# TensorE turns the identity 80 times behind each count of tokens and 16 times at the head of each expert stage, results unread

## What is computed

```python
def _L0_ffn_ref(x, router_w, w1, b1, w2, b2):
    logits = jnp.einsum('td,ed->te', xf, router_w)
    top_vals, top_idx = jax.lax.top_k(logits, K)
    probs = jax.nn.softmax(top_vals, axis=-1)
    for e in range(E):
        w = jnp.sum(jnp.where(top_idx == e, probs, 0.0), axis=-1)
        h = jax.nn.gelu(jnp.einsum('td,fd->tf', xf, w1[e]) + b1[e], approximate=False)
        y = jnp.einsum('tf,df->td', h, w2[e]) + b2[e]
        out = out + w[:, None] * y
...
x = x + 0.5 * _L0_ffn_ref(_layernorm(x, axis=-1), ...)
x = x + _L0_attn_ref(_layernorm(x, axis=-1), ...)
x = x + 0.5 * _L0_ffn_ref(_layernorm(x, axis=-1), ...)
...
```

## Time and profile before

| what | value |
|---|---|
| median of 3 runs | 2718.38 us (2714.81, 2718.38, 2722.18) |
| the profiled execution's own time | 2709.58 us |
| its span, first to last instruction | 2707.7 us |
| mean granted TensorE clock over the span | 0.926 |
| TensorE (PE) busy | 2202.2 us, 81% of the span |
| VectorE (DVE) busy | 1953.2 us, 72% |
| ScalarE (ACT) busy | 1418.8 us, 52% |
| GpSimd (POOL) busy | 941.5 us, 35% |
| instructions | 48032 |

### The profile page before, as it was taken

The page is one execution under the profiler, slowest core; times in us unless marked ns, Lnnn a source line. Parts: engine busy times, 40 slices in busy tenths (PEclk is TensorE's granted clock), DMA queues, the critical chain, the costliest instruction groups (busy, mean ns, idle before and its releaser), DMA issues. The chain is left out here.

```text
span 2707.7 us, 48032 instructions
## 1 busy us (share of the span) xinstructions
PE 2202.2 (81%) x15540; PEld 1400.0 (52%) x15540; DVE 1953.2 (72%) x4474; ACT 1418.8 (52%) x2911; POOL 941.5 (35%) x1180
## 2 busy tenths in 40 slices
PE   3399788866978779999999997859776697698986
PEld 3299576756965312232322324659756696433334
DVE  3466688865655679999999974556587565688893
ACT  2166222214645459989899893236443464533333
POOL 4444345553442421111111102554446444223330
PEclk9999898977989969999999998879987798899998
DMA  5122100001220230000000001112211123100001
GB/s 171 40 60 65 50 23 18 17 24 48 66 83 32 83 113 22 21 22 23 20 23 22 20 2 39 35 49 66 64 58 37 56 65 86 46 0 0 0 1 32
DMA packets 110499, 115.42 MB, mean 43 GB/s; under 512 B 21776, under 2 KB 93552, under 8 KB 109488
## 3 DMA queue, kind: packets, MB, share of 16 engines
q1 hardware_dynamic: 91936, 76.13, 9.7%
q0 software_dynamic: 17280, 35.69, 3.9%
q10 hardware_dynamic: 1040, 0.53, 0.1%
HBM read 67.30 MB, written 44.57 MB: 41 GB/s over the span
## 5 line engine op out<-in xcount | busy, mean ns | idle before, releaser
L2060 DVE TENSOR_REDUCE attn_nm<-bank 128x1 f32<-128x1024 f32 x512 | 592.4, 1217 | 27.2 <-PE bank L1802 24.9
L1924 ACT ACTIVATE attn_pT<-bank 128x512 f32<-128x512 f32 x1024 | 554.3, 597 | 64.6 <-PE bank L1818 57.8
L1802 PE MATMUL bank<-attn_K,attn_Q 48*128 48x512 bf16 x1024 | 317.8, 391 | 23.3 <-PEq L1536 16.6
L1837 PE MATMUL bank<-attn_pT,attn_vb 128*32 128x256 f32 x4096 | 328.2, 391 | 10.4 <-issue 10.4
L1818 PE MATMUL bank<-attn_Q,attn_K 51*128 51x512 bf16 x1024 | 318.8, 384 | 1.5 <-DMA attn_Q<-attn_m_parts 1.4
L2004 POOL CAST attn_m_cols<-attn_nm 128x8 bf16<-128x8 f32 x64 | 12.2, 191 | 482.2 <-DVE attn_nm L2060 454.7
L1802 PEld LDWEIGHTS bank<-attn_K,attn_Q 48*128 48x128 bf16 x1024 | 59.2, 94 | 230.8 <-DVE attn_nm L2060 143.0
L1837 PEld LDWEIGHTS bank<-attn_pT,attn_vb 128*32 128x32 f32 x4096 | 82.1, 108 | 185.1 <-issue 135.3
L2873 POOL TENSOR_TENSOR mix_rS<-mix_rT,mix_S 128x512 f32<-128x512 f32 x64 | 82.8, 1293 | 171.2 <-DVE mix_S L2928 83.9
L1023 PE MATMUL bank<-mix_prod_qk,ident 128*128 128x256 f32 x512 | 122.8, 394 | 0.9 <-issue 0.7
L1023 PEld LDWEIGHTS bank<-mix_prod_qk,ident 128*128 128x128 f32 x512 | 102.0, 200 | 31.8 <-issue 18.6
(11 more groups left out here) (617 smaller groups left out, 5688.8 us busy)
## 6 DMA issues: line engine op xcount, KB each, us to landing
w<-in_L_w SPq DMA_DIRECT2D x4, 2048.0 KB
ffn0a_x_ring<-xs_rows SPq DMA_DIRECT2D x71, 65.0 KB
ffn0b_x_ring<-xs_rows SPq DMA_DIRECT2D x71, 65.0 KB
ffn2a_x_ring<-xs_rows SPq DMA_DIRECT2D x71, 65.0 KB, 1.8
ffn2b_x_ring<-xs_rows SPq DMA_DIRECT2D x71, 65.0 KB, 1.8
mix_in_y_back<-y_rows SPq DMA_DIRECT2D x8, 512.0 KB
ffn1a_in_y_back<-y_rows SPq DMA_DIRECT2D x8, 512.0 KB, 4.0
decay_in_y_back<-y_rows SPq DMA_DIRECT2D x8, 512.0 KB
```

The lines of the kernel that those rows point to most:

```text
L1802: ins = nc.tensor.matmul(out[:, hf, :], slot(net.Q, h, 0, KROWS)[:, qt * P:(qt + 1) * P], slot(net.K, h, 0, KROWS)[:, hf * CH:(hf + 1) * C ...
L1837: ins = nc.tensor.matmul(pv_bank[at:at + VCOL, cols], vb[:, h, kt, :], q[:, cols], start=(opens(h) and pair == 0 and half == 0), stop=(clo ...
L1924: nc.scalar.activation(pT[:, p_at(b, h, kt), hf * CH:(hf + 1) * CH], s_bank(n), ACT.Exp, scale=HD ** -0.5).then_inc(s_used, 1)
L2060: nc.vector.tensor_reduce(nm[:, v % NMRING, qt:qt + 1], a_bank(n).rearrange("p a t -> p (a t)"), AX.X, ALU.max, negate=True).then_inc(a_us ...
```

## The change

A helper is added that has TensorE transpose the identity into the first 128 columns of a bank a number of times. Norm.count calls it with bank 6 and 80 times, behind its product and behind a wait for kept that covers all chunks. moe_stage calls it with bank 6 and 16 times ahead of turn(0). Nothing reads the results, and no semaphore is raised by them. count runs four times and moe_stage four times, so 384 transposes are added.

```diff
+def turn_nothing(nc, net, bank, times):
+
+    for _ in range(times):
+        nc.tensor.transpose(bank[:, 0:P], net.ident[:], net.ident[:])
...
@@ class Norm, count
         self.nc.tensor.matmul(self.rbank[:, 2 * P:2 * P + E], self.net.ones[:], self.net.taken[:], start=True,
                               stop=True).then_inc(self.counted, 1)
+        pe.wait_ge(self.kept, NCH)
+        turn_nothing(self.nc, self.net, self.tbank, 80)
...
@@ moe_stage, block.tensor
+            turn_nothing(nc, net, net.bank[6], 16)
             turn(0)
             turn(1)
             for s in range(SLOTS + 2):
```

## The result

The changed kernel takes 2724.78 us (median of 20 runs, 2713.86 to 2736.62), the kernel before 2715.23 us on the same chip (median of 20 runs, 2703.82 to 2732.47). The ratio is 1.0035, with a 95% interval of 1.0018 to 1.0052: slower by 0.35%, some 9.5 us (4.9 to 14.1). Forecast was 0.24% faster. The profiled execution has a span of 2725.0 us.

The account below looks back on a forecast made before the run. TensorE, busy 81% of the span, was taken to bound the expert stages, their heads running at half clock. Heads gain 6.9 us, less 0.5 us for lost clock: 2718.38 - 6.4 = 2712.0 us, range 2705 to 2722.

Parts of the forecast that it names:

- the cost of the 80: Behind each count: 80 transposes take 10.8 to 12.1 us, hidden behind GpSimd's scatters, cost 0.
- The price of one: One added transpose, start to start: 0.213 us at the low clock, 0.11 us at the full one.
- The cover: GpSimd's time from the count to VectorE's release, hiding the 80: 12.6, 12.2, 13.9 and 13.9 us.
- The heads: Expert stages, turn(0) to first down: at the full clock they gain 6.9 us in all.
- The 16: Ahead of turn(0): 1.75 us at full clock, cost 0; at the low clock heads start about 0.7 us later.
- The clock lost in the waits: Between the 80 and the 16 in ffn2a and ffn2b, waits of 1.8 to 3.1 us sometimes lose the clock: 0.5 us off.
- Do transposes lift the clock?: The whole gain hangs on transposes raising TensorE's clock; the trace leaned towards yes, the Trainium skill page said no.
- The first: Rival at the blocks' ends: all 80 run slow, TensorE late by 15.8 us, heads stay slow; 2737 us, chance 0.09.
- The second: Rival at the heads: clock lost again, or slot loads take over; gain 0 to 3 us, 2717 us, chance 0.15.
- The third: Rival at the heads: all slow time is halved and kept, 9.7 us gained; 2708.7 us, chance 0.14.

Follow-up runs that it names:

- e6: Changed kernel, but the 80 transposes wait until all scattered rows have landed; 2714.56 us against 2669.08 for the kernel before.
- e10: Changed kernel, but the scatters of the last two chunks of mix are issued in one row of 16; 2725.60 us.
- e5: Changed kernel with 10 products over 512 columns in place of the 80 transposes, the 16 kept; 2660.53 us, ratio 0.9971 to the kernel before.
- e9: Changed kernel with 20 products over 512 columns in place of the 80 transposes; 2734.61 us.
- e3: Changed kernel with 40 products of the identity with itself (80 pairs) in place of the 80 transposes; 2718.97 us, ratio 1.0052 to the kernel before.
- e4: Changed kernel, but the 80 transposes write the four quarters of bank 6 in turn; 2715.84 us, ratio 1.0035 to the kernel before.
- e1: Changed kernel without the 16 transposes, only the 80 kept; 2722.54 us, ratio 1.0066 to the kernel before.
- e2: Changed kernel without the 80 transposes and the added wait, only the 16 kept; 2704.95 us, ratio 0.9997 to the kernel before.
- e11: Changed kernel with 11, 10, 12 and 12 products over 512 columns in place of the 80 transposes; 2701.61 us, ratio 0.9973 to the kernel before.
- e8: Changed kernel with 20 products over 256 columns (40 pairs) in place of the 80 transposes; 2664.91 us.
- e7: Changed kernel with 36 transposes behind the count in place of 80; 2666.90 us, ratio 0.9992 to the kernel before.

## Why the prediction was wrong

**The step that failed** is the cost of the 80: "All of 10.8 to 12.1 fit, the tightest by 0.1 us. Cost 0." It cost 14.8 us. The price of one was right: steps of 0.213 us at the low clock and 0.109 at the full one, 15 slow ones in the load stage and 20 in mix (23 forecast), and 11.04 us for the 80 in mix (11.2 forecast). The cover was right too: GpSimd comes to the block's end 12.75, 12.44, 14.03 and 14.14 us behind the count, and did so 12.75, 12.36, 14.01 and 14.21 us behind it before. Only its last 0.3 us weren't free, since VectorE's first instruction comes 0.42 us behind the last engine's end and not 0.1; at the long end of the forecast, 12.1 us, the 80 would have been late in mix by some 0.1 us. What the step left out is that the cover isn't empty time. It is GpSimd's scatters, and 160 narrow instructions beside 12 or 16 of them in a row don't run at TensorE's pace: from the 40th or about the 60th transpose on, one takes 0.6 to 1.4 us on average in place of 0.109. The prediction had the place for it, in "No row shows a cost of fetching instructions on TensorE; I take 0, since at either clock they run while it would idle, and the rivals bound it". No row could show it: nowhere in the trace of before does TensorE have a dense row of instructions beside those scatters, and a cover that has never been used in this way should have had a rival of its own.

**Shown** are these conditions: scatters beside the run (e6), a row of them that is longer than eight and begins ahead of the count (e10), narrow instructions in great number or close upon each other (e5 and e9 against e3), and neither the kind of instruction nor the place of its result (e3, e4), nor the 16 (e1). Of e6, e9 and e10 there is one execution each, but the six kernels with 80 narrow pairs beside the scatters agree: all stop in the load stage, ffn1b and decay, and in mix e10 alone. **Open** is the mechanism. The steps of 0.7 us, and the end of the stop near GpSimd's last scatter, look like TensorE's supply of instructions waiting behind the scatters' own traffic; but the recorded instruction fetches of TensorE don't line up with the stop (one lies 4.3 us behind the count in the load stage and another 7.5 us ahead of it in ffn1b), and no run took that path away. That these fetches are TensorE's is read from their number: 132 packets of 16 KB on that queue before, and 135 with 768 more instructions of TensorE. Nor was it tried what lies between 8 and 12 scatters, or many narrow instructions set apart from each other.

**The heads** were right: forecast 1.4, 2.2, 1.65 and 1.65 us, 6.9 in all; measured 1.36, 2.23, 1.46 and 1.45, 6.5. Down starts 4.57 and 4.50 us behind turn(0) (4.5 forecast) and 4.00 and 3.97 (3.8 forecast). The table load for the gelu is what is late next, as said: it starts 2.5 us behind turn(0).

**The 16** cost nothing at the full clock, as forecast (1.94 us at three places). In ffn2b they begin at the low clock and take 2.71 us; turn(0) follows them at once there, 2.61 us behind VectorE's first instruction against 2.50 before. Their price at the low clock, 0.7 us of a later turn(0), is measured by e2: 0.5 to 0.9.

**The clock lost in the waits** was put at 0.5 us. After, it wasn't lost over any head, but only because TensorE itself is late and the wait is 0.4 us at three places. The worry was sound: 3.63 us of waiting lose it in e5, 1.34 to 2.2 us don't in e11, nor do 2.51 us in e8 (ffn2a, 1.94 us for the 16).

**Do transposes lift the clock?** They do. In mix TensorE has nothing but transposes behind the count, and the clock goes from 0.50 (627.90 to 632.80) to 1.00 (633.20 on); in e6, where they follow 18.7 us of idle, 80 take 11.37 us, nearly as quick as in mix. So the page "TensorE: Matmul & The Clock Gate" of the Trainium skill, section "Part 4: PE-mode transpose", by which they aren't counted as busy and the full clock doesn't engage, doesn't hold here; by it the 80 would have taken 17.1 us, late at all four places, mix among them.

**The rivals.** The first named the right symptom, TensorE late at the end of the block, and its 2737 us is nearer to 2724.8 than the forecast; but its mechanism (slow clock throughout, heads slow, mix worst) isn't what happened. The second is what the heads of e1 and e7 show. The third is out, since the heads gained what the forecast said. The range, 2705 to 2722, ended below the result because it left the failing step without a bound: the prediction had bounded the added instructions by nothing but their clock.

With the step mended, the rest of the sum stands. By the same table, e11 gives +1.3 us for the blocks and -6.7 for the heads, -5.3 in all, and it measures 0.27% (0.03 to 0.51), some 7.3 us: faster than both kernels, by about what was forecast for the change. Where the profile's sum and the measured ratio differ (8.3 and 9.5 after, 5.3 and 7.3 in e11), the intervals are wider than the difference, and no run settles it.

## What to carry to other kernels

An engine's idle time beside another engine's transfers isn't free cover for any filler: bound the filler with the work that it runs beside, and look in the profile after for gaps with "issue" in the middle of a row of equal instructions. To keep TensorE's clock over a pause, use few wide products and not many narrow ones, fit their length to the wait at each place, and keep the idle time before the real work short (here 2.5 us kept the clock and 3.6 us lost it). When a change does what it should in one place and loses in another, cut it in two and vary only its form: e11 keeps the whole gain by a wider operand, in a number fitted to each place.

## What was unexpected in the hardware

- 80 pairs of weight load and product over 128 columns, beside a row of 12 or 16 indirect scatters of 1.27 us each, fall to starts that are mostly 0.7 us or a multiple of it apart (on average one instruction in 0.7 us in the load stage, one in 0.4 us in ffn1b, decay and e10's mix). It begins at the 40th to 43rd pair where the row began 8.6 us ahead of the count, at the 58th to 65th where it began 2.4 us ahead, and TensorE picks up again 0.3 to 1.3 us behind the time at which GpSimd has come to the end of its list. VectorE's and GpSimd's instructions keep their steps meanwhile (in the load stage VectorE's table takes 7.5 us with the 80 and without; GpSimd's scatters stay 1.27 us apart).
- Beside a row of eight the same 80 take 11.04 us without a gap, and 40 pairs over 512 columns go without a gap beside a row of 8, 12 or 16 (19.59 us in mix).
- Transposes of float32 alone bring the clock from 1.2 to 2.4 GHz, after 12 to 27 steps of 0.213 us, and a pause of 1.34 us ahead of the 16 keeps it (1.94 us for the 16, e11), one of 3.63 us doesn't (3.27 us, e5).
